# Layer-0 FFN rows: the product with the gate moved from GpSimd to ScalarE in chunks 5 and 6

## The reference, cut to what matters

```python
xn = _layernorm(x)
x = x + _L0_attn_ref(xn, ...) + _L0_ffn_ref(xn, ...)      # layer 0
xn = _layernorm(x)
x = x + _L1_attn_ref(xn, ...) + _L1_ffn_ref(xn, ...)      # layer 1

# in _L0_ffn_ref: every token goes to one of 8 experts, at most 256 tokens each
gates = softmax(x @ wg); idx = argmax(gates)
expert_out = gelu(dispatched @ w1 + b1) @ w2 + b2
out[token] = gate[token] * expert_out[row of the token]   # 0 where the expert was full
```

## Time and profile before

| what | value |
|---|---|
| median of 3 runs | 373.73 us (372.53 to 373.87) |
| the profiled execution | 372.24 us, its span 370.4 us |
| TensorE busy | 318.9 us, 86% of the span |
| VectorE busy | 233.0 us, 63% |
| ScalarE busy | 180.0 us, 49% |
| GpSimd busy | 152.1 us, 41% |
| mean granted TensorE clock | 0.967 of full speed |
| chain that ended last, by engine | PE 69%, DVE 14%, issue 6%, ACT 5%, DMA 4%, POOL 1% |

### The profile page before, as it was taken

The page is one execution under the profiler, slowest core; times in us unless marked ns, Lnnn a source line. Parts: engine busy times, 40 slices in busy tenths (PEclk is TensorE's granted clock), DMA queues, the critical chain, the costliest instruction groups (busy, mean ns, idle before and its releaser), DMA issues.

```text
span 370.4 us, 11512 instructions
## 1 busy us (share of the span) xinstructions
PE 318.9 (86%) x4024; PEld 276.5 (75%) x4024; DVE 233.0 (63%) x722; ACT 180.0 (49%) x517; POOL 152.1 (41%) x203
## 2 busy tenths in 40 slices
PE   0867899999999899896878979999999999999800
PEld 0556677878998778675655569999999999999800
DVE  4758878782115699997588868875664444444416
ACT  1536466466556665646358633333334444444304
POOL 9130774010001787430122264545458875543320
PEclk9999999999999999999899699999999999999975
DMA  7990114002651101012011368788788888997046
GB/s 222 354 317 10 45 45 135 13 2 73 178 159 30 51 23 45 4 58 87 32 58 56 127 213 275 249 235 260 229 264 272 295 277 280 295 282 250 26 128 226
DMA packets 36664, 57.23 MB, mean 155 GB/s; under 512 B 4320, under 2 KB 15904, under 8 KB 36608
## 3 DMA queue, kind: packets, MB, share of 16 engines
q1 hardware_dynamic: 31840, 46.14, 40.2%
q0 software_dynamic: 4192, 9.31, 7.7%
q10 hardware_dynamic: 576, 1.05, 0.9%
HBM read 46.59 MB, written 9.90 MB: 152 GB/s over the span
## 4 chain that ended last, share of the span: by engine, by line
PE 69%; DVE 14%; issue 6%; ACT 5%; DMA 4%; POOL 1%; SPq 1%; ACTq 0%; DVEq 0%; POOLq 0%
PE bank L1297 19%; PE bank L1279 9%; PE bank L1306 4%; PE bank L1085 4%; PE bank L1071 4%; PE bank L1005 3%; PE bank L978 3%; DVE rmax L1501 3%; PE bank L858 2%; DVE shared L1505 2%; DMA cb<-in_cb 2%; PE bank L1028 2%; PE bank L1252 1%; PE bank L925 1%; PE bank L905 1%
## 5 line engine op out<-in xcount | busy, mean ns | idle before, releaser
L1297 PE MATMUL bank<-kf,shared 128*128 128x128 f32 x624 | 76.1, 275 | 0.0
L1297 PEld LDWEIGHTS bank<-kf,shared 128*128 128x128 f32 x624 | 73.3, 192 | 0.4
L543 POOL DMA_INDIRECT y_rows<-rows,to x39 | 39.0, 999 | 49.7 <-DVE rows L1755 48.3
L832 ACT ACTIVATE we<-bank,bcol 128x128 f32<-128x128 f32 x78 | 24.4, 363 | 53.6 <-PE bank L1297 53.6
L1747 DVE SCALAR_TENSOR_TENSOR we<-bank,bcol,we 128x128 f32<-128x128 f32 x78 | 23.7, 346 | 40.2 <-ACT we L832 40.1
L537 POOL DMA_INDIRECT rows<-xn_rows,from x39 | 37.6, 965 | 19.1 <-issue 11.3
L1279 PE MATMUL bank<-xtT,shared 128*128 128x128 f32 x312 | 41.4, 276 | 0.9 <-ACT xtT L800 0.7
L1279 PEld LDWEIGHTS bank<-xtT,shared 128*128 128x128 f32 x312 | 38.0, 192 | 1.5 <-ACT xtT L800 0.9
L1501 DVE TENSOR_REDUCE rmax<-bank 128x8 f32<-128x512 f32 (+2 forms) x48 | 30.1, 628 | 13.3 <-PE bank L978 10.4
L817 ACT ACTIVATE kexp<-bank,bcol 128x128 f32<-128x128 f32 x78 | 24.4, 363 | 29.0 <-PE bank L1279 29.0
L1726 DVE SCALAR_TENSOR_TENSOR kf<-bank,bcol,kexp 128x128 f32<-128x128 f32 x78 | 23.9, 347 | 20.6 <-ACT kexp L817 19.6
(11 more groups left out here) (249 smaller groups left out, 643.2 us busy)
## 6 DMA issues: line engine op xcount, KB each, us to landing
shared<-in_w1s SPq DMA_DIRECT2D x39, 512.0 KB, 4.7
shared<-in_w1s SPq DMA_DIRECT2D x39, 256.0 KB, 4.2
we<-in_we SPq DMA_DIRECT2D x8, 514.0 KB, 3.6
xn_rows<-xn SPq DMA_DIRECT2D x8, 256.0 KB, 2.3
x<-in_x SPq DMA_DIRECT2D x4, 256.0 KB, 3.5
xs_rows<-kf POOLq DMA_DIRECT2D x4, 256.0 KB, 7.7
y_rows<-kf POOLq DMA_DIRECT2D x4, 256.0 KB, 10.4
w1s<-in_w1s SPq DMA_DIRECT2D x2, 512.0 KB, 15.0
```

What stands on the lines that cost most here:

```text
L543: pool.indirect_dma_start(out=y1_rows, in_=ysb[:, i % 4, :], in_offset=None, out_offset=bass.IndirectOffsetOnAxis(ap=to1[:, i:i + 1].bitca ...
L832: last = act.activation(sil2[:, (k - 1) % 2, a, :], bank[(1, 3)[(k - 1) % 2]][:, P * a:P * a + P], ACT.Silu, bias=bias(e, 4 + a))
L1297: mm = pe.matmul(bank[(1, 3)[(k - 1) % 2]][:, P * f:P * f + P], wglb[:, (k - 1) % 4, a, P * f:P * f + P], zT2[:, (k - 1) % 2, a, :], start ...
```

## The change

The product leaves `add_rows`. ScalarE gets a new function `gated_rows(i)`, which waits for the four gathers of group `i` and multiplies the four tiles one by one with the gate of their rows. It is called twice in chunk 5 (groups 0 and 1) and twice in chunk 6 (groups 2 and 3), once ahead of `exponent(g + 2)` and once behind it. GpSimd now waits for ScalarE's fourth product and only adds.

```diff
             def add_rows(n, i):
                 tiles_ = slice(4 * i, 4 * i + 4)
-                pool.wait_ge(s_y0[i], 64)
-                pool.tensor_tensor(xn[:, tiles_, :], xn[:, tiles_, :], gate[:, tiles_].unsqueeze(2).broadcast_to([P, 4, P]), ALU.mult).then_inc(s_gated, 1)
                 pool.wait_ge(s_gated, i + 1)
                 pool.wait_ge(s_x1, n - 1)
                 pool.tensor_tensor(x[:, tiles_, :], x[:, tiles_, :], xn[:, tiles_, :], ALU.add).then_inc(s_added, 1)
+            def gated_rows(i):
+                act.wait_ge(s_y0[i], 64)
+                for t in range(4 * i, 4 * i + 4):
+                    last = act.activation(xn[:, t, :], xn[:, t, :], ACT.Copy, scale=gate[:, t:t + 1])
+                last.then_inc(s_gated, 1)
...
                     query_heads(n + 1)
+                if n in (BACK, BACK + 1):
+                    gated_rows(2 * (n - BACK))
                 exponent(g + 2)
+                if n in (BACK, BACK + 1):
+                    gated_rows(2 * (n - BACK) + 1)
                 weighted(n, 0)
                 weighted(n, 1)
                 gates(n)
```

## The result

| what | before | after |
|---|---|---|
| median of 17 executions each | 373.56 us (371.5 to 374.65) | 378.35 us (374.69 to 384.59) |
| ratio after / before | | 1.0122, 95% interval 1.0093 to 1.0151 |
| the profiled execution, its span | 372.24 us, 370.4 us | 379.56 us, 377.7 us |
| mean granted TensorE clock of it | 0.967 | 0.958 |
| ScalarE, GpSimd busy | 180.0, 152.1 us | 184.9, 147.9 us |

The kernel is 1.2% slower: by the ratio 4.6 us, by the two medians 4.8.

A forecast was written before the change was run, and what follows sets the result against it. It took a chain through ScalarE's tanh, TensorE and VectorE to bound chunks 5 and 6, with GpSimd off it. Chunk 5's +2.35 and chunk 6's +1.25 make +3.6 us on 373.73, so 377.3 us, range 375.4 to 379.3.

The forecast's parts named there:

- The positions that it named: Chunks 5 to 7: L1035 at about 139.0, L1501 at 141.9, chunk 6's L1035 at 155.4, chunk 7's L1501 at 165.1.
- The sign of being wrong: Wrong if chunk 5's L1035 moves under 2 us, chunk 7 starts under 3 or over 4.2 late, or the rest changes over 1.
- ScalarE is on the chain between L616 and L646 in chunk 5, and all of the new work counts: Chunk 5, ScalarE ahead of L646: no gap there, so both calls delay TensorE's L1035 and VectorE's chain by 2.35 us.
- The price of a call: ScalarE, each call of gated_rows: four activations of 0.29 us, together 1.17 us, so 2.35 us per chunk.
- Chunk 6 meets slack: Chunk 6: the second 2.35 us meets waits of 1.1 us in all, so it costs +1.25 us.
- VectorE's freed time is worth nothing here and 0.6 us if ScalarE is off the path: VectorE in chunk 6: L1513 is no longer stretched by GpSimd, a gain of 0.6 us there, but 0 in the sum.
- The adds that stay cost nothing: GpSimd's adds L487 move behind the products; at worst they take about 1.2 of VectorE's 1.85 us in hand, cost 0.
- The wait for gathered rows costs nothing: ScalarE's new wait before the products: group 3's rows land at 148.5, needed at 153.4, 4.9 us to spare, cost 0.
- rival D: TensorE's clock falls behind the new gap ahead of L1035: about +1.2 us more, 378.5 us; chance 20%.
- C: Nothing hides the new work in chunks 5 and 6: +4.7 us, 378.4 us; chance 12%.
- Rival A: The eight activations per chunk fit into ScalarE's idle time, not slower: 373.1 us, at best 372.5; chance 8%.
- B: Chunk 6 hides its part: only +2.35 us, 376.1 us; chance 17%.

The follow-up runs named there:

- e3_warm: The changed kernel with extra matmuls that nobody needs filling TensorE's gaps in chunks 5 and 6; 375.75 us, ratio 1.0090 to the kernel before.
- e5_idle2: e4_idle with GpSimd's last add held until VectorE has made mix of chunk 5; 372.08 us, ratio 0.9973 to the kernel before.
- e4_idle: The changed kernel with ScalarE's products moved to where it waits for TensorE, GpSimd's order following; 373.82 us, ratio 1.0044 to the kernel before.
- e10_warm_again: e3_warm run once more, beside the changed kernel on one chip; 377.01 us, ratio 1.0133 to the kernel before.
- e6_warm7: The kernel before with 10 extra matmuls filling TensorE's wait of 2.58 us in chunk 7; 370.82 us, ratio 0.9948.
- e2_only6: The changed kernel with the product on ScalarE in chunk 6 alone, chunk 5 keeping GpSimd's product; 374.61 us, ratio 1.0053 to the kernel before.
- e9_after_again: The changed kernel itself run once more on one chip; 378.34 us, ratio 1.0179 to the kernel before.
- e11_warm6: The changed kernel with only TensorE's gap of chunk 6 filled by extra matmuls; 375.41 us, ratio 1.0108 to the kernel before.
- e8_double5: e3_warm with each product of chunk 5 made twice and 22 instead of 11 extra matmuls there; 379.23 us, ratio 1.0156 to the kernel before.

## Why the prediction was right, step by step

- *The positions that it named.* The forecast took a steady clock, so e3_warm is the run to hold it against. Its first mark lies 0.92 us later than that of before; with this taken off, the turn of chunk 5 begins at 138.97 (forecast 139.0), the maximum behind it at 141.86 (141.9), the turn of chunk 6 at 155.37 (155.4) and the maximum of chunk 7 at 164.94 (165.1).
- *The sign of being wrong.* The prediction said that it is wrong if the start of chunk 7 is late by more than 4.2 us. In the profiled execution of the kernel after it is 6.64 us late, so by this sign the forecast failed for that execution, and the windows name the reason, as it said they would: the clock, in both chunks. In e3_warm it is 3.42 us late, inside the bounds.
- *ScalarE is on the chain between L616 and L646 in chunk 5, and all of the new work counts.* Right: 2.35 us were forecast for chunk 5; 2.30 were read in e3_warm, and the doubled dose added 2.35.
- *The price of a call.* Right: 1.17 us per four products, as in the kernel after.
- *Chunk 6 meets slack.* Right in kind, 0.2 us too small in size: 1.1 us of slack were counted and 1.28 found (2.35 - 1.07), so this term was 1.07 us and not 1.25. By the distances from the first mark in e3_warm, the turn absorbed 0.28 instead of 0.23 us, the way on to L884 0.77 instead of 0.64, the last L973 0.24 instead of 0.23.
- *VectorE's freed time is worth nothing here and 0.6 us if ScalarE is off the path.* Right: L1521 is back at 0.42 us in the kernel after, while VectorE waits 1.98 us for TensorE at the second mark in e3_warm and 2.94 in the kernel after; e5_idle2, where ScalarE is off the path, gains 0.56.
- *The adds that stay cost nothing.* Right for the time. The prediction looked only at instructions with two SBUF inputs, and in chunk 6 an add stretched another kind: the `var` instruction, 0.17 to 0.43 us. VectorE had the time in hand. In e4_idle it had not, and the same pairing cost 1.1 us.
- *The wait for gathered rows costs nothing.* Right: no wait of ScalarE for a gather stands in the profile.
- *The clock, rival D, with a chance of 20%.* This was mis-sized. It was kept out of the forecast as a rival with one fall of 1.2 us behind the gap of chunk 5. Measured are falls behind both gaps, 1.3 to 1.6 us each, in some executions and not in others. With two falls the path's 3.4 us become the 6.6 of the profiled execution. The median of all executions lies between, at 378.35, which is D's 378.5 and C's 378.4 as much as the forecast's 377.3: that it fell inside the range is in part luck, since it hangs on how many executions had a fall. How much of the 4.6 us is falls isn't shown by the times either, for e10_warm_again, with none in its profiled stretch, lay 4.8 us above its own kernel before. Two falls explain 3.2 us of the scatter of 10; the executions of 381 us and more have a mean clock of 0.943 to 0.950, below the 0.958 of the profiled one with its two falls, so they had more than these, and where and why stays open. The sum without falls, +3.6, was within 0.2 us of the path's cost.
- *Rival A, ScalarE has room.* It has, elsewhere: e5_idle2 puts the same sixteen products into its waits at no cost. At the place of the change it has none.
- *Rivals B and C.* With no fall chunk 6 costs 1.1 us, where B has 0 and C 2.35.

## What to carry to other kernels

A half idle engine has room only where it waits: find the instruction on the chain that the new work is put in front of, and the new work costs its full length until the first slack behind it, wherever that is. Instructions of GpSimd and VectorE must be placed against each other as well, since a short instruction of VectorE can be held for the whole of a long one of GpSimd, as in e4_idle (1.29 beside 1.27 us). A new wait of 2 to 3 us in TensorE's work cost a second time through the clock in some executions here; look for the falls in the windows before judging by a few executions. Filling the wait removed the falls from every profiled stretch; by the times only the filled wait of chunk 7 shows a gain (e6_warm7, 0.5%).

## What was not expected of the hardware

- The clock fell behind gaps of 1.95 us (kernel after and e2_only6, chunk 6) and 2.82 us, but not behind the 1.95 us of e9_after_again (chunk 6) or the 2.83 us of e11_warm6. The slower clock lasted about 3.4 us each time in chunks 5 and 6 and cost 1.3 us (e9_after_again, where it began with the turn itself at 137.6 us) to 1.6 us on the path (in the kernel after it began 1.9 us behind the turn of chunk 5). The second chunk of e3_warm, e8_double5 and e10_warm_again has a fall from about 40 us on that the other profiles lack, with nothing changed there; in e3_warm the waits of TensorE just ahead of it are 0.92 and 0.67 us.
- GpSimd holds not only VectorE instructions with two SBUF inputs, as its product did with L1513 (1.38 instead of 0.42 us). Its add also held one with a single SBUF tensor of 8 elements per partition: 1.29 instead of 0.17 us. The Trainium skill (GPSIMD Engine Reference, Key points) names contention with instructions in a two-port mode beside those with two inputs; this agrees with it, if that instruction ran in such a mode, which no run here shows.
- GpSimd's add itself took 1.33 us in the kernel before and 1.27 us in the kernel after. What accounts for the 0.06 us was not tried.
